# Second layer's VectorE order, the step between the layers, and three small moves in the first layer

## The reference

```python
xn = _layernorm(x, axis=-1)
x = x + _L0_attn_ref(xn, ...) + _L0_ffn_ref(xn, ...)
xn = _layernorm(x, axis=-1)
x = x + _L1_attn_ref(xn, ...) + _L1_ffn_ref(xn, ...)
```

```python
left, right = x @ compare_left, x @ compare_right          # 256 x 64 each
comparison = einsum('bik,bjk->bij', left, right) / sqrt(256)
attn = (comparison > threshold) * softmax(comparison + gate_bias) @ x
xr, xk = mu_r * x + (1 - mu_r) * x_prev, mu_k * x + (1 - mu_k) * x_prev
ffn = sigmoid(xr @ W_r.T) * (relu(xk @ W_k.T) ** 2 @ W_v.T)
```

## Time and profile before

| | |
|---|---|
| median of 3 runs | 1025.79 us (1025.3 to 1028.23) |
| profiled execution | 1024.89 us, span 1023.0 us |
| TensorE busy | 976.5 us (95%), 7956 matmuls |
| VectorE busy | 836.0 us (82%) |
| ScalarE busy | 748.0 us (73%) |
| GpSimd busy | 766.1 us (75%) |
| granted TensorE clock | 1.00 in every slice |
| first layer's ring ends, second layer's bodies begin | about 842 us, about 858 us |

### The profile page before, as it was taken

How to read it: one execution, slowest core, us unless ns; L and a number is a source line. 1 busy time by engine, 2 the same in 40 slices (tenths; PEclk the granted TensorE clock), 3 DMA queues, 4 the chain that set the end, 5 groups by cost and what they waited for, 6 DMA issues and landing times.

```text
span 1023.0 us, 23654 instructions
## 1 busy us (share of the span) xinstructions
PE 976.5 (95%) x7956; PEld 672.4 (66%) x7956; DVE 836.0 (82%) x2272; ACT 748.0 (73%) x1998; POOL 766.1 (75%) x942
## 2 busy tenths in 40 slices
PE   5889989999999999999999999999999998999998
PEld 4556655766666666666666666666666665776776
DVE  7989988788889888878788778877778757999885
ACT  5989987667766677676767666766766766988984
POOL 3777768778778787878787778777878545878885
PEclk9999999999999999999999999999999999999999
DMA  8733534243443333333333333333333101111111
GB/s 266 244 115 121 154 113 150 82 133 109 125 113 92 108 103 93 94 113 95 95 98 119 103 95 96 120 106 94 94 94 94 53 1 27 35 35 35 48 54 43
DMA packets 102903, 101.32 MB, mean 99 GB/s; under 512 B 13952, under 2 KB 98560, under 8 KB 102144
## 3 DMA queue, kind: packets, MB, share of 16 engines
q1 hardware_dynamic: 102784, 99.81, 32.1%
HBM read 56.25 MB, written 40.90 MB: 95 GB/s over the span
## 4 chain that ended last, share of the span: by engine, by line
PE 70%; DVE 15%; ACT 6%; issue 3%; POOL 3%; DMA 2%; SPq 0%; DVEq 0%; ACTq 0%; POOLq 0%
PE bank L1664 22%; PE bank L1761 12%; PE bank L1747 12%; PE bank L1778 8%; PE bank L1735 6%; PE bank L1736 5%; PE bank L1905 2%; DVE arena L1369 2%; ACT arena L890 2%; PE bank L1965 2%; POOL arena L646 2%; DVE arena L1385 1%; DVE arena L1533 1%; DMA arena<-in_weights 1%; DVE x_sb L1555 1%
## 5 line engine op out<-in xcount | busy, mean ns | idle before, releaser
L646 POOL TENSOR_SCALAR arena<-arena,rc 128x128 f32<-128x128 f32 (+3 forms) x512 | 278.7, 562 | 177.9 <-DVE rc L1378 177.0
L890 ACT ACTIVATE arena<-arena,nm 128x256 f32<-128x256 f32 (+3 forms) x512 | 284.7, 556 | 111.6 <-DVE nm L1369 107.2
L1369 DVE CUSTOM_DVE_ANT_0 arena<-bank,mask_rows 128x256 f32<-128x256 f32 (+3 forms) x512 | 233.1, 484 | 87.5 <-PE bank L1736 82.4
L1747 PE MATMUL bank<-ident,arena 128*128 128x128 f32 x1280 | 211.9, 278 | 12.6 <-DVE arena L1385 5.1
L1747 PEld LDWEIGHTS bank<-ident,arena 128*128 128x128 f32 x1280 | 149.7, 141 | 72.6 <-DVE arena L1385 29.8
L1736 PE MATMUL bank<-arena 128*128 128x256 f16 (+3 forms) x512 | 152.9, 299 | 0.0
L1761 PE MATMUL bank<-arena 128*64 128x512 f32 (+3 forms) x1024 | 152.0, 439 | 0.0
L1735 PE MATMUL bank<-arena 128*128 128x256 f16 (+3 forms) x512 | 139.9, 300 | 1.3 <-DMA arena<-scr 1.3
L1761 PEld LDWEIGHTS bank<-arena 128*64 128x64 f32 x1024 | 67.9, 136 | 94.7 <-issue 69.8
L1385 DVE COPY arena<-bank 128x512 f32<-128x512 f32 (+3 forms) x256 | 124.8, 487 | 3.7 <-PE bank L1747 3.3
L898 ACT ACTIVATE arena<-bank 128x512 f32<-128x512 f32 (+3 forms) x256 | 108.8, 425 | 14.5 <-PE bank L1747 13.9
(11 more groups left out here) (183 smaller groups left out, 2163.1 us busy)
## 6 DMA issues: line engine op xcount, KB each, us to landing
arena<-scr SPq DMA_DIRECT2D x320, 128.0 KB, 2.7
scr<-arena SPq DMA_DIRECT2D x256, 128.0 KB, 1.7
arena<-in_weights SPq DMA_DIRECT2D x5, 1024.0 KB, 7.7
x_sb<-in_x SPq DMA_DIRECT2D x8, 512.0 KB, 8.8
out<-x_sb SPq DMA_DIRECT2D x16, 256.0 KB, 2.2
xscr<-arena SPq DMA_DIRECT2D x12, 256.0 KB, 3.0
arena<-wh SPq DMA_DIRECT2D x40, 64.0 KB, 2.0
xsh<-xscr SPq DMA_DIRECT2D x6, 256.0 KB, 3.5
```

The lines of the kernel that those rows point to most:

```text
L646: last = pool.tensor_scalar(pr[slot][:, OFF[i]:OFF[i + 1]], pr[slot][:, OFF[i]:OFF[i + 1]], rc[:, slot, i:i + 1], 1.0, ALU.mult, ALU.mult)
L890: act.activation(pr[slot][:, OFF[i]:OFF[i + 1]], pr[slot][:, OFF[i]:OFF[i + 1]], ACT.Exp, scale=-1.0, bias=nm[:, slot, i:i + 1], accum_out ...
L1369: dve.tensor_tensor_reduce(pr[slot][:, OFF[i]:OFF[i + 1]], s_tile[i], mask_rows[:, SQ - P * (i + 1):SQ], -1.0, -MASKED, ALU.add, ALU.min, ...
L1747: last = pe.transpose(banks[5 + h][:, (i - j) * P:(i - j + 1) * P], pr[2 * par + h][:, OFF[i] + j * P:OFF[i] + (j + 1) * P], ident[:])
```

## The change

- ScalarE, first layer: the high parts of the output weights are made in steps 7 and 8, not 6 and 7.
- VectorE, first layer: `row_maximum(7)` goes ahead of `out_low(6)`; the column maximum and scale of the output weights go from the end of step 5 into the middle of step 6; `sc_vo`, the product of two scales, goes from step 6 to step 8.
- The passage: VectorE does `ffn_part(7, 0)` ahead of `out_low(63)` and of two memsets, and `side_low(0)` ahead of `mix_all(0, 1)`; ScalarE does the transposed rows of batch 0 ahead of the normalised rows of batch 1; TensorE has `sides` after three pairs of the first half (not four), and `compare` after two pairs of the second half (not four).
- Second layer, ScalarE: `top_bias(n + 1, 1)` ahead of `side_high(n + 2)`.
- Second layer, VectorE: `pt3_low(n + 1, 0)` and `(n + 1, 1)` ahead of `mix_all(n + 2, 2)` and `rows_high(n + 2)`; part 0 of the roots after body 0, part 1 after body 1, parts 2 and 3 after body 2.

```diff
-                elif n in (6, 7):
+                elif n in (7, 8):
                     act.wait_ge(setup_done, 3)
-                    for c in (2 * n - 12, 2 * n - 11):
+                    for c in (2 * n - 14, 2 * n - 13):
...
+                if n == -2:
+                    normalised(1, range(NT))
                 mix_high(n + 1, 3)
                 pt3_high(n, 3)
                 receptance_tanh(n + 1, 0, 1 - u)
                 if n >= -1:
                     normalised(n + 3, (0, 1))
+                top_bias(n + 1, 1, 1 - u)
                 side_high(n + 2)
-                top_bias(n + 1, 1, 1 - u)
...
-            normalised(1, range(NT))
...
                 elif n == NB - 1:
-                    row_maximum(n)
...
-                elif n == 6:
+                elif n == 8:
                     dve.tensor_tensor(sc_vo[:], sc[:, G_V:G_V + 1], sc[:, G_O:G_O + 1], ALU.mult)
...
-                if n == 5:
-                    column_maximum(slice(G_O, G_L), 2)
-                    weight_scale(slice(G_O, G_L), 2)
-                elif n == 7:
+                if n == 7:
...
                 maxima(n + 1, 0, e, (1,))
+                if n == NB - 1:
+                    row_maximum(n)
                 out_low(n - 1)
...
                     part_maximum(n - 1)
+                elif n == 6:
+                    column_maximum(slice(G_O, G_L), 2)
+                    weight_scale(slice(G_O, G_L), 2)
...
-            out_low(NR - 1)
...
-            dve.memset(xf3[:, :, 0:1], 0.0).then_inc(xf3_zero, 1)
-            dve.memset(rl3[L:P], 0.0).then_inc(rl3_zero, 1)
...
                 final(n, 1, u)
-                rows_high(n + 2, u)
-                mix_all(n + 2, 2)
                 pt3_low(n + 1, 0)
                 pt3_low(n + 1, 1)
+                mix_all(n + 2, 2)
+                rows_high(n + 2, u)
                 top(n + 2, 0, u)
 
             ffn_part(NB - 1, 0, wo)
+            out_low(NR - 1)
+            dve.memset(xf3[:, :, 0:1], 0.0).then_inc(xf3_zero, 1)
+            dve.memset(rl3[L:P], 0.0).then_inc(rl3_zero, 1)
             xt_low3(0, 0)
             xt_low3(0, 1)
             ffn_part(NB - 1, 1, pj)
             mix_all(0, 0)
+            side_low(0)
             mix_all(0, 1)
-            side_low(0)
...
                 if n < 1:
                     row_statistics(NB - 1 + n)
-                elif n < 3:
-                    roots(last_two, 3, (2 * n - 2, 2 * n - 1))
-                if n == 2:
+                if 0 <= n < 2:
+                    roots(last_two, 3, (n,))
+                elif n == 2:
+                    roots(last_two, 3, (2, 3))
                     roots_bias(last_two)
...
-            attended(NB - 1, 0, (0, 1, 2, 3), wo)
+            attended(NB - 1, 0, (0, 1, 2), wo)
             sides(0, (xt3l_done, 2, 0, 0))
-            attended(NB - 1, 0, (4, 5, 6, 7), wo)
-            attended(NB - 1, 1, (0, 1, 2, 3), pj)
+            attended(NB - 1, 0, (3, 4, 5, 6, 7), wo)
+            attended(NB - 1, 1, (0, 1), pj)
             compare(0, 0, (lrl_done, 1, 0, 0))
             compare(0, 1, (xt3l_done, 2, 0, 1))
-            attended(NB - 1, 1, (4, 5, 6, 7), pj)
+            attended(NB - 1, 1, (2, 3, 4, 5, 6, 7), pj)
```

## The result

The changed kernel takes 1031.97 us (median of 6 runs, 1030.84 to 1033.26); the kernel before, beside it, 1024.91 (6 runs, 1023.64 to 1028.23). The ratio is 1.0065, 95% interval 1.0051 to 1.0078: slower, 2 us above the forecast's figure and just past the upper end of its range (1031.9). The profiled execution took 1032.36 us, its span 1030.3, 7.3 longer than before's.

A forecast was written before the change was run, and what follows sets the result against it. TensorE was taken to bound the first layer, a chain through VectorE's tail, ScalarE and `gated` the second. Terms of -1.9 + 0.5 - 0.5 + 2.6 + 0.5 + 1.15 + 1.9 = +4.25 gave 1030.0 us, range 1024.5 to 1031.9.

The forecast's parts named there:

- Pairs 6 and 7, -1.9: First layer: moved VectorE and ScalarE work removes TensorE's idle time in these head pairs, 1.9 us faster.
- Passage, +0.5: Between the layers: TensorE waits less for `ffn_part`, but then for `xt_low3` and the moves; `gated` 0.5 us later.
- `top_bias`, -0.5 in body -1 and 0 elsewhere: Second layer: exponentials 0.4 us earlier save 0.5 before batch 0; elsewhere `mix_all` still starts behind GpSimd's `mix_before`.
- Bodies 3 to 5, +2.6: VectorE's tail: `key_low` goes before the cast in five of six, `top` ends 1.04 us later; 3 x 0.87.
- Roots of body 0, +1.9: End of body 0: three added operations, each held by one of GpSimd's, make `gated` start 1.9 us later.
- Roots of body 1, +0.5: End of body 1: three cheap operations leave, saving 0.6; the others meet GpSimd's work 1.15 later; 0.5 us slower.
- of body 2, +1.15: End of body 2: the roots end behind GpSimd's shifted work, 1.15 us slower.
- The shift of GpSimd's work: Second layer: the moved mix and cast delay GpSimd's following work by 1.15 us in every body, 0.65 in body 0.
- VectorE keeps the port: Rival, chance 0.22: mix and cast run back to back, `key_low` waits, bodies 3 to 5 cost nothing; 1027.4 us.
- `mix_all` ahead of `mix_before`: Rival, chance 0.08: `mix_all` gets the port first, `final` and `top` end 0.4 earlier in bodies 0 to 5; 1020.2 us.

The follow-up runs named there:

- e1: Changed kernel with the roots again as before (parts 0 and 1 after body 1, 2 and 3 after body 2); 1028.82 us, 1.0038 of before.
- e3: Kernel before with the first layer's moves alone; 1022.99 us, 0.9983 of before.
- e8: Kernel before with the first layer's moves and roots behind `gated(n + 1, 1)`: part 0 body 1, part 1 body 2, parts 2 and 3 body 3; 1023.04 us.
- e9: e8 with `top_bias` ahead of `side_high` and the new passage with one more pair ahead of the comparison; 1019.1 us, 0.9943 of before.
- e11: Changed kernel with its roots placed as in e8, behind `gated(n+1,1)` of bodies 1, 2 and 3; 1023.81 us, 0.9988 of before.
- e6: Kernel before with the new order of the passage between the layers alone; 1025.89 us, 1.0008 of before.
- e5: Kernel before with `top_bias(n + 1, 1)` ahead of `side_high(n + 2)` alone; 1024.68 us, 0.9996 of before.
- e2: Kernel before with the two low parts ahead of `mix_all(n + 2, 2)` and `rows_high(n + 2)` alone; 1029.3 us, 1.0045 of before.
- e7: Kernel before with the roots' split alone (part 0 after body 0, part 1 after body 1, parts 2 and 3 after body 2); 1026.52 us, 1.0015.
- e10: Kernel before with the edits of e2 and e4: low parts first, whole roots behind `gated(n+1,1)` in bodies 1 and 2; 1026.08 us, 1.001.
- e12: Kernel before with whole roots behind `gated(n+1,1)` in bodies 1 and 2, and `top_bias` ahead of `side_high`; 1022.44 us, 0.9976 of before.
- e4: Kernel before with the roots of bodies 1 and 2 moved behind `gated(n + 1, 1)`, ahead of `gate_value`; 1024.02 us, 0.9989 of before.

## Why the prediction came out as it did

The sign and most of the mechanisms held; the sum of +4.25 fell short of the measured difference (7.1 between the medians, 6.7 by the ratio, 5.85 in the trace without the start). The steps that it lists measured +2.8, and one that it doesn't list +3.1. That 1030.0 lies within 2 us of the measured 1031.97 is in part luck: steps put 1.4 too high and a starting point of 1025.79, 0.9 above the median of six runs, make up for most of the term that is missing.

- **Pairs 6 and 7, -1.9:** right. -1.8 in the change, in e1, e3, e8, e9 and e11. In pair 6 0.69 of idle time remains, where the working left 0.44, and of pair 7's 1.21 nothing, where it left 0.05.
- **Passage, +0.5:** right in size and mechanism: +0.50 in e6. By starts the waits for `xt_low3` and for the moves are 0.31 and 0.77, for 0.3 and 0.8. e9 shows that the pair missing between the moves and the comparison is the cause: with it the order gains 0.15.
- **`top_bias`, -0.5 in body -1 and 0 elsewhere:** body -1 gained 0.75 in e9; in the changed kernel only 0.14, since the low parts' order let `key_low` hold the cast for 1.65 there (at 871.81, as in body 3), which the forecast did not count. Elsewhere the first mix began 0.56 sooner (2.14 ahead of the second `key_relu`, 1.58 in before), not 0.4. In bodies 2 and 4 `mix_before` took most of that back, as forecast: `final` began 0.05 and 0.04 after `key_relu`, 0.12 and 0.10 in before. In bodies 1, 3 and 5 it did not: one of the two mixes was not held (0.74; in 1 and 3 the second `mix_before` began early, 2.27 ahead of `key_relu`), and `final` began 0.46 ahead of `key_relu`, 0.56 to 0.59 sooner than in before. In e5, with this edit alone, `final` came at most 0.15 sooner; in e2, without it, 0.4 in bodies 2 to 5. So that gain is not this edit's alone.
- **Bodies 3 to 5, +2.6:** the mechanism is there, the size is not. Bodies 3, 4 and 5 pay +0.47, -0.15 and +0.44 once the clock's part is off, 0.8 together. Two reasons. `key_low` got ahead of the cast in bodies -1, 1, 3 and 5 and stayed behind in 0, 2 and 4, not five in six; and where it did (cast +0.97), the sooner `final` had already gained 0.5: `top` starts 4.64 after `key_relu` in bodies 3 and 5, 4.07 in body 4, 4.12 to 4.16 in before.
- **Roots of body 0, +1.9:** +2.3, by the mechanism named, though two operations were held and not three: the last ends at 898.14, where `mix_low` ends (895.98 + 2.14). e7, without GpSimd's shift, has +1.5.
- **Roots of body 1, +0.5:** +0.14; **of body 2, +1.15:** +1.08. Right in kind, with the first of body 2 held for 2.02, by `rows_low`. The shift of GpSimd's work, put at 1.15 everywhere, was 1.1 in body 2 and 0.76 in body 1 (`rows_low` against the second `key_relu`), where `key_low` did not wait for the cast; less the 0.6 of three cheap operations that is the 0.14.
- **Not in the sum: the granted clock, +3.06** in the profiled execution (1.67 + 1.39). The forecast worked out by how much `gated` would be late and counted each us once; but TensorE's own wait grew to 2.36 and 3.03, and products behind it ran at 1.2 GHz. In e1 and e2 it is the larger part of the loss: 3.3 and 3.05 us. The medians say that it is no accident of one execution. The mean granted clocks of the changed kernel's six runs are 0.993 to 0.997, median 0.995 (one fall takes about 1.7 us of 1030, 0.0017; a third fall of the profiled execution lies in the start, near 47 us). Of 92 runs of before taken with the experiments the median is 0.998, and 28 show 1.000. By those 92 a thousandth of mean clock goes with 0.8 us (28 runs at 1.000: median 1023.80; 10 at 0.996: 1026.91), which makes 2.3 us of the three thousandths between the medians. This goes by runs side by side: none held the clock up under the same waits, so the share of the clock is read from traces, not switched.

Of the rivals, "VectorE keeps the port" was true of every second body, and "`mix_all` ahead of `mix_before`" came true in e9, in bodies 1 to 3, where it was worth 0.5 a body. A loss was forecast for the reasons that hold: held root operations and a shifted `key_low`. What the forecast had as its largest term measured a third of that, and the one that it left out was the largest.

Open: why the cost of the new order moves from body to body. The tie at the port (below) tells who goes first, but where GpSimd stands at that moment depends on the bodies before, and that chain was not followed through all of them. One more tie takes part: in body 3 of before the second mix is held by `mix_before` (1.09) and `top` starts 4.16 after `key_relu`, in e3, with the same code there, it takes 0.75 and `top` starts at 3.76. What sets the spread of the start and its falls of the clock was not tried either.

## What to carry to other kernels

A tiny operation costs what it has to wait for. Put it where the other engine on the same port is known to be idle, and see what stands right behind it: taking seven operations of 0.17 out of the tail was worth 1.4 us there and cost 0.8 at the new place, three cost 0.15. Before pricing a delay at its own length, add up the wait of TensorE that it makes: here the falls of the clock behind waits of 2.36 us and more cost 1.4 to 1.7 us each, beside delays of 1 to 2. And take a bundle apart: one part of this one gained 1.8, one 0.75 in one body and 0.5 in three more once its neighbours let it, one turned from +0.5 to -0.15 by one pair of heads, and the two that lost outweighed them all.

## What the runs showed of the hardware

**Who gets the port.** The tails of five kernels with the new order (changed, e1, e2, e10, e11; seven bodies each) give 35 ties between GpSimd's `key_low` and VectorE's mix (0.74) with the cast right behind it. Asking 0.03 to 0.43 after the mix began (21 cases), `key_low` waited for mix and cast; asking 0.50 or 0.51 after it (12), it waited for the mix alone and went ahead of the cast; asking 0.35 ahead of it (2), it went first. So two VectorE operations back to back can keep the port although GpSimd asked during the first, and a later request, not an earlier one, got between them. Later still it is open: in body -1 of the nine kernels with the old order, `key_low` asks 0.57 after the second mix began and 0.09 or 0.10 ahead of the cast. In six it waited for the cast (before: `key_low` at 869.64, 1.79 long, cast 0.69); in three, e8, e9 and e12, it went first. In e9:

```profile
867.02 1.19 POOL L725 TENSOR_TENSOR arena<-arena 128x512 f16<-128x512 f32 x1 [2.58 <-ACT arena L1032]
867.11 1.64 DVE L1493 CAST arena<-arena 128x1024 f16<-128x1024 f32 x1
```

The Trainium skill, page "SBUF — State Buffer", section "SBUF: two separate sides", says that of a GpSimd operation and a VectorE operation in a two-port mode or with two SBUF inputs, whichever starts first gets the shared pair for its whole instruction. The lengths here agree (1.35, 1.65, 2.25 are own length plus the other's rest). Read as in the prediction, that the first to ask goes first, it does not fit: the cast of bodies 0, 2 and 4 started after `key_low` had asked and was not held.

**Not every small operation is held.** `gated`'s reciprocal of 128 x 1 takes 0.16 in e4 at 916.05, in the middle of GpSimd's `mix_low` (915.04 to 917.17), beside which root operations of 128 x 8 took 1.01 in the changed kernel.

**Equal waits, with and without a fall of the clock.** Waits of 2.36, 2.75, 2.76, 2.95, 2.96 and 3.03 us ahead of `turn` were followed by a fall, one of 2.06 was not, and of those of 1.65 near 858 us, one in each of the 14 profiles, some were (e5, e7, e8, e10, e12) and some not (before, changed, e1 to e4, e6, e9, e11). A fall in the second layer cost 0.96 to 1.67 us.
